# Edge sums of a relational network: from one stream on 125 weight columns to two streams on blocks of 64 and 61

## The reference

```
def _mgcn_conv(x, edge_index, edge_type, rel, W_in, W_out, W_loop, b, n):
    src, dst = (edge_index[0], edge_index[1])
    e = edge_index.shape[1]; half = e // 2
    m = x[src] * rel[edge_type]
    m = jnp.concatenate([m[:half] @ W_in, m[half:] @ W_out], 0)
    deg = jax.ops.segment_sum(jnp.ones((e,), x.dtype), dst, num_segments=n)
    norm = 1.0 / jnp.maximum(deg, 1.0)
    agg = jax.ops.segment_sum(m * norm[dst][:, None], dst, num_segments=n)
    return jnp.tanh(agg + x @ W_loop + b)
h = emb + res * _mgcn_conv(emb, ..., rel1, W_in1, W_out1, W_loop1, b1, n)
h = h + res * _mgcn_conv(h, ..., rel2, W_in2, W_out2, W_loop2, b2, n)
gnn = h @ mu_w + mu_b
...
xn = _layernorm(x)
x = x + gnn(xn, src, dst, edge_type) + mix(xn)   # mix: 4 layers of linear attention and a 256-1024-256 FFN
x = x + ffn(_layernorm(x))                       # shared MLP plus 4 experts, the best 2 weighted
```

## Time and profile before

| | |
|---|---|
| median of three runs | 1943.48 us |
| span of the profiled execution | 1937.8 us |
| TensorE busy | 1821.0 us (94%) |
| GpSimd busy | 1322.3 us (68%) |
| VectorE busy | 1248.8 us (64%) |
| ScalarE busy | 632.8 us (33%) |

### The profile page before, as it was taken

How to read it: one execution, slowest core, us unless ns; L and a number is a source line. 1 busy time by engine, 2 the same in 40 slices (tenths; PEclk the granted TensorE clock), 3 DMA queues, 4 the chain that set the end, 5 groups by cost and what they waited for, 6 DMA issues and landing times.

```text
span 1937.8 us, 28847 instructions
## 1 busy us (share of the span) xinstructions
PE 1821.0 (94%) x9176; PEld 1505.8 (78%) x9176; DVE 1248.8 (64%) x3345; ACT 632.8 (33%) x1552; POOL 1322.3 (68%) x1301
## 2 busy tenths in 40 slices
PE   2899899999899999999999789998899999999999
PEld 1567787887588888768888667876788888888998
DVE  6786465674855576486466645868765666654766
ACT  4452233343323333332333222332121211223443
POOL 6777777777777777777777757777777777770000
PEclk9999999999999999999999989999999999999999
DMA  9568666667776666687677856667766766661000
GB/s 274 177 198 258 203 191 206 186 202 222 243 209 199 204 194 198 208 249 214 193 218 220 274 190 229 190 200 224 229 182 215 209 199 200 190 181 17 15 28 28
DMA packets 194575, 371.44 MB, mean 192 GB/s; under 512 B 37993, under 2 KB 126095, under 8 KB 194430
## 3 DMA queue, kind: packets, MB, share of 16 engines
q0 software_dynamic: 77632, 223.91, 40.6%
q1 hardware_dynamic: 92228, 126.68, 19.9%
q10 hardware_dynamic: 24570, 19.04, 3.4%
HBM read 305.39 MB, written 64.95 MB: 191 GB/s over the span
## 4 chain that ended last, share of the span: by engine, by line
PE 80%; DVE 8%; issue 3%; DMA 3%; POOL 2%; SPq 2%; ACT 2%; DVEq 0%; ACTq 0%
PE ps_down L2765 16%; PE ps_hid L2753 16%; PE ps_seg L2629 15%; PE ps_kv L2662 5%; PE ps_x L2717 4%; PE ps_x L546 3%; PE ps_hid L3229 2%; PE ps_kv L3082 2%; POOL xg L959 2%; PE ps_hid L2682 1%; DVE xg L1055 1%; PE ps_kv L2795 1%; PE ps_down L2795 1%; DMA h_rows<-qT_all 1%; PE ps_hid L3220 1%
## 5 line engine op out<-in xcount | busy, mean ns | idle before, releaser
L959 POOL DMA_INDIRECT xg<-h_rows,idx_tab x416 | 437.2, 1051 | 143.3 <-issue 114.0
L906 POOL DMA_INDIRECT rg<-relation_rows,idx_tab x416 | 426.7, 1026 | 133.5 <-issue 126.1
L959 POOL DMA_INDIRECT xg<-xn_rows,idx_tab x416 | 423.4, 1018 | 131.9 <-issue 120.3
L2629 PE MATMUL ps_seg<-xg,hot 128*125 128x257 f32 x1664 | 414.8, 382 | 19.7 <-DVE xg L1055 19.5
L2753 PE MATMUL ps_hid<-hT,wff 128*128 128x250 f32 (+1 forms) x1920 | 368.3, 341 | 1.0 <-issue 0.8
L2629 PEld LDWEIGHTS ps_seg<-xg,hot 128*125 128x125 f32 x1664 | 305.3, 188 | 75.0 <-DVE xg L1055 19.2
L2765 PE MATMUL ps_down<-wff,gT 128*125 128x256 f32 x1600 | 363.6, 381 | 0.0
L2753 PEld LDWEIGHTS ps_hid<-hT,wff 128*128 128x128 f32 x1920 | 312.8, 189 | 37.9 <-issue 7.9
L1055 DVE TENSOR_TENSOR xg<-xg,rg 128x512 f32<-128x512 f32 x416 | 285.8, 687 | 70.8 <-DMA rg<-relation_rows,idx_tab 52.0
L2765 PEld LDWEIGHTS ps_down<-wff,gT 128*125 128x125 f32 x1600 | 295.2, 188 | 41.3
L2204 ACT ACTIVATE gT<-ps_hid,b1p 128x250 f32<-128x250 f32 (+1 forms) x480 | 177.8, 433 | 291.6 <-PE ps_hid L2753 291.5
(11 more groups left out here) (378 smaller groups left out, 2385.5 us busy)
## 6 DMA issues: line engine op xcount, KB each, us to landing
second_relation_rows<-rg SPq DMA_DIRECT2D x104, 512.0 KB, 4.1
rg<-second_relation_rows SPq DMA_DIRECT2D x104, 512.0 KB, 4.1
wff<-L_mix_W ACTq DMA_DIRECT2D x8, 1024.0 KB
rg<-relation_rows,idx_tab POOLq DMA_INDIRECT x416, 3.5
xg<-xn_rows,idx_tab POOLq DMA_INDIRECT x416, 3.2
xg<-h_rows,idx_tab POOLq DMA_INDIRECT x416, 3.6
h_rows<-qT_all SPq DMA_DIRECT2D x25, 112.0 KB
qrow<-h_rows ACTq DMA_DIRECT2D x25, 112.0 KB
```

The costliest lines, as they stand in the source:

```text
L906: pool.indirect_dma_start(rg[:, k, :], None, rel_d, bass.IndirectOffsetOnAxis(ap=idx_tab[:, step, 1:2], axis=0))\
L959: pool.indirect_dma_start(xg[:, k, 0:D], None, rows, bass.IndirectOffsetOnAxis(ap=idx_tab[:, step, 0:1], axis=0))\
L2629: ins = pe.matmul(ps_seg[u // UW % 2][0:T, 0:AW], hot[:, s % HOTS, :], xg[:, s % RING, :], start=s % WIN == 0, stop=s % WIN == WIN - 1)
```

## The change

The edges are cut into two streams, the first and the second half of the list (208 steps each). The nodes are cut the same way: tile t now holds 64 nodes of a first strip (nodes 64t on) and 61 of a second (1600 + 61t on), so that stream one fills partitions 0 to 63 of a tile and stream two partitions 64 to 124. A unit is four steps, two of each stream, and each step's one-hot is 64 columns wide. TensorE sums a pair of steps by two matmuls one behind the other, one with 64 weight columns to the lower partitions, one with 61 to the upper ones (L2735). For the nodes in which the streams overlap, 12 steps of a layer get one more matmul (L2740).

With it change: windows of 6 pairs and 97 masked adds a layer in place of 104, plus one plain one, at row numbers known when the program is built (no loads of row numbers); one-hots and products of four steps in one VectorE instruction each (208 and 208 where there were 416 and 416); a slot of the ring is released after four steps, not two; the relations are reloaded 4 blocks ahead, not 8; the tile products become two loop matmuls over the full width and four over the strips (L3190, L3193); rows move in three DMAs, not two; x comes back by a load and a VectorE add, so no `add_x` is left on GpSimd.

The order changes too: the passage stands behind (2,3), one group later, with 6 units (24 steps) among its tiles, behind every third; the second network layer starts with (2,4), and its last 104 steps are doled out over the experts' slots 1 to 12; 18 of the product slots move behind layer 3 as well, to the experts' slots 1 to 16.

```
-UNIT = 2
-WIN = 8
+UNIT = 4
+HOT_UNITS = 2
+WIN = 6
+STRIPS = ((0, 64), (64, T))
...
-STEPS_JOINT = (14, 14, 14, 36)
-STEPS_GROUP = ((20, 26, 24, 24, 24), (20, 24, 24, 24, 22), (18, 24, 68, 48, 54), (58, 58, 58, 56, 48))
-AMONG, AMONG_AT = 20, 2
-DENSE_LAYER, DENSE_GROUP = 2, 3
+STEPS_JOINT = (16, 16, 16, 32)
+STEPS_GROUP = ((16, 24, 24, 24, 24), (16, 24, 24, 24, 24), (16, 24, 24, 48, 48), (24, 52, 52, 52, 52))
+STEPS_LAST = 104
+AMONG, AMONG_AT, AMONG_EVERY = 6, 3, 3
+DENSE_LAYER, DENSE_GROUP = 2, 4
+LAG = 18
...
# TensorE, one unit
-                    for s in range(u * UNIT, (u + 1) * UNIT):
-                        ins = pe.matmul(ps_seg[u // UW % 2][0:T, 0:AW], hot[:, s % HOTS, :], xg[:, s % RING, :],
-                                        start=s % WIN == 0, stop=s % WIN == WIN - 1)
+                    for i in range(PER):
+                        now = u * PER + i
+                        for j, (a, z) in enumerate(STRIPS):
+                            part = j * PER + i
+                            ins = pe.matmul(ps_seg[bank_of(w)][a:z, 0:AW], hot[:, u % HOT_UNITS * UNIT + part, 0:z - a],
+                                            xg[:, u % RU * UNIT + part, :], start=now == r, stop=now == end - 1)
...
# TensorE, one tile's product
-                for k in range(n):
-                    ins = pe.matmul(out_rows, sums(k), weights[k // KC](k % KC), start=k == 0, stop=k == n - 1)
+                for c in range(KC):
+                    pe.matmul(bank_rows(0, T), sums(KC + c), wg[g][2][:, c, :], start=c == 0, stop=False)
+                for c in range(KC):
+                    for j, (a, z) in enumerate(STRIPS):
+                        ins = pe.matmul(bank_rows(a, z), sums(c)[:, a:z], wg[g][j][:, c, :], start=False, stop=c == KC - 1)
...
# the experts' slots on TensorE
+                for slot in slots[:len(slots) // 2]:
+                    dense_beside(slot)
...
+                upto(last_units(s, 0))
                 if s < NT:
                     experts_1(s)
...
+                upto(last_units(s, 1))
+                for slot in slots[len(slots) // 2:]:
+                    dense_beside(slot)
```

827 lines of the change are left out of this document (466 added, 361 removed).

## The result

The changed kernel takes 1985.66 us (median of four runs, 1978.38 to 1990.71) against 1942.67 for the kernel before: ratio 1.0233, 95% interval 1.0202 to 1.0265 (the quotient of the two medians is 1.0221). It is slower; 1859 was forecast, in a range from 1832 to 1925. The profiled execution is the slowest of the four, with a span of 1988.9 us.

What follows compares the result with a forecast made beforehand. TensorE was taken as the bound, with GpSimd equally pacing the first layer. Passage ends 1168, layer 3 starts 1286, experts 1609, slot 12 ends 1754, then 99: span 1853, plus 5.7 gives 1859 us; range 1832 to 1925.

Steps and rivals of the forecast that it cites:

- A step on TensorE: Edge matmuls on two column blocks: overlap makes a four-step unit take 1.08 us, 0.27 a step, where it was 0.435.
- First-layer gathers end at 1133: First network layer: GpSimd issues the same 832 gathers, so the last one ends at 1133 us as before.
- What costs nothing: List of edits taken as free, among them four-step one-hots and products on VectorE, saving time that nobody waits for.
- TensorE reaches the passage at 1078: Passage behind (2,3): TensorE gets there at about 1078 us, when GpSimd, at 1069, has 24 first-layer steps left.
- (2,4) 107: Group (2,4) with the joint: 85.5 us without edges plus 80 steps at 0.27 makes 107 us.
- layer 3 323: Mix layer 3, from 1286 to 1609 us: five groups sum to 315 us, with 8 added for waits.
- slots 1 to 12 145: Experts' slots 1 to 12: 130 us of TensorE work plus 15 us of waits, slot 12 ending at 1754.
- GpSimd is ahead by less than its ring: Start of the experts: TensorE arrives at 1609 us, and GpSimd has step 312 there at 1599.
- x's way back and the third DMA: x's DMAs leave GpSimd's queue, about 2 us each; each row move's third DMA, on SyncE's queue, is covered by the passage.
- No overlap: Rival: blocks do not overlap, a unit costs 1.74 us as before, extra matmuls add 53 us: 1997 us; chance 0.13.
- the first rival: Partial overlap, 0.35 us a step, or 0.217 us pauses between blocks and full width: 1905 us; chance 0.17.
- VectorE's edge work in the experts: Rival: VectorE and the experts' banks set slots 1 to 12, uncovered products and one-hots cost 43 us: 1902; chance 0.11.

Runs made afterwards that it cites:

- e6: Changed kernel with VectorE's product of a unit in two instructions of two steps instead of one of four: 1954.69 us, ratio 1.0091 to the kernel before.
- e8: Changed kernel with no edge steps beside the experts; layer 3's groups carry 64 and four times 68 steps: 2055.22 us, ratio 1.0603 to the kernel before.
- e13: e6 with second-layer gathers fetching 64 rows in place of 128: 1956.70 us, ratio 1.0111 to the kernel before.
- e4: Kernel before the change with units of four steps in place of two, no column blocks: 2042.79 us, ratio 1.0574 to the kernel before.
- e3: Changed kernel with units of two steps in place of four, and with them the product in two: 1991.26 us, ratio 1.0293 to the kernel before.
- e14: e3 with 56 steps beside the experts in place of 104, the others moved to layer 3: 1971.02 us, ratio 1.0163 to the kernel before.
- e17: Changed kernel; at layer 3's start ScalarE loads x and one h tile first, other tiles behind its first gelus: 1979.99 us, ratio 1.0198 to the kernel before.
- e18: Changed kernel with the edits of e6 and e17, layer 3's steps at even places and three units of one-hots: 1939.94 us, ratio 0.9998 to the kernel before.
- e1: Changed kernel with loops over steps and blocks exchanged in unit and tile product, same block's matmuls in succession: 1977.53 us, ratio 1.0218 to the kernel before.
- e5: Changed kernel with every edge and strip matmul over the full width, no blocks, same number of matmuls: 2052.64 us, ratio 1.0595 to the kernel before.
- e10: e6 with rows moved in two DMAs of 64 and 61 rows in place of three: 2189.34 us, ratio 1.1311 to the kernel before.

## Why the prediction was wrong

- **A step on TensorE: the size right, the mechanism not.** 1.02 to 1.11 us for the forecast 1.08. The forecast was five lengths of 0.216, with one block's first pass beside the other's second; the records show four, with both blocks' passes side by side, and some 0.09 us at each change of width, 0.18 a unit, which the sum put at nothing. That the two errors cancel is luck. The reading of the earlier trace rows went wrong because a modelled end behind the next start says nothing of a pause: the unit at 343.65 has such an end too (344.74, the next start 344.67), and the pause is there. The Trainium skill (TensorEngine Tiling (Array Packing), Key Properties) has a drain at each change of tiling mode, and this trace agrees that a change costs something, with 0.31 where 0.216 is usual.
- **First-layer gathers end at 1133: wrong, 1155.9.** The step that failed stands under "What costs nothing": the four-step product "saves VectorE time that nobody waits for". Nobody waits for it, but its length holds GpSimd's gathers up (e6), and GpSimd set the first layer's pace: the earlier trace rows had told that. 17 of the 23 us are longer gathers (437.7 and 429.5 us busy for 423.4 and 426.7). I costed the edit by its engine, not by what else its instruction touches.
- **TensorE reaches the passage at 1078, 8 us behind GpSimd: wrong, 1120** (1097 in e6). 21 to 23 us are the gathers. The rest is lag: TensorE starts its first group at 183.3 in place of 168.3, and at 63.06 busy of 64.60 us a group, with GpSimd at 24 x 2.69 = 64.6 (1.052 and 1.033 and two issues of 0.30 a step), it can't catch up. The passage itself took 83 us, 90 forecast; it ended at 1203, not near 1168, which was one of the signs named for being wrong. The first gather behind it came after 6.4 us, not 4.
- **(2,4) 107, layer 3 323, slots 1 to 12 145, the end 99 us: measured 127, 377, 156 and 113** (to the end of the span). PE busy is 109, 333, 140 and 98. In (2,4) the 107 held 9 us of idle time of the kernel before, and left out the 12 extra matmuls of a layer (L2740), which stand there: 24 instructions, some 5 us. In layer 3 the work was put at 315; a good part of the difference is the clock of 0.95, at which the FFN's 880 matmul instructions of this layer take 195.1 us (before, at 1.00, 185.2). The rest is idle time. What failed is the step "GpSimd is ahead by less than its ring", by which TensorE would hardly wait. By my own numbers 52 steps are 71 us on GpSimd, and TensorE needed 70.2: two engines with equal work, coupled by a ring of four units and by VectorE's order. GpSimd waited 84 us for slots, VectorE 58 for second-layer gathers (of the 129 us ahead of L1143), TensorE 44 in layer 3, some 24 of them behind a late gather. I added 8. That the equal pace makes them wait is argued from these rows and from e8; no run changed GpSimd's pace in the second layer (e13 hardly did). "Up to two steps longer" for the coarser release was the wrong measure too, if e4's 110 us, part of them by the long product, are a guide; in the changed kernel e3 and e14 don't show such a cost.
- **x's way back and the third DMA: mis-costed.** I looked at GpSimd's queue and SyncE's; eight of the 18 issues that stand ahead of the gelu are new ones on ScalarE's (x15 was x10, and x3 is new), and x is now waited for on VectorE. e17 and e18 put the place at 0.0035, 7 us.
- **The clock: not in the sum.** After 9 us of idle time TensorE came back at about half its clock, 0.54, as the rows of the changed kernel under e17 show; the FFN's matmuls of the whole kernel, whose number is the same, take 744 us in the changed kernel and 732 before.
- **The rivals.** No overlap is excluded (e1, e5). A pause at each change of width is real, but 0.09 us where the first rival took 0.217, and paid for by the fuller overlap. VectorE's edge work in the experts is real with units of two (e3, e14). With units of four the 15 us of waits added to slots 1 to 12 were about right (16.4 idle), though 9.6 of them are for the norm and only 5.1 for edge products; the 11 us beyond the forecast are busy time, at a clock of 0.93. What came true was not among the rivals: none asked what the change does to GpSimd's pace and to its coupling with TensorE, and "slower" had 0.13, all of it for no overlap.

A small slip in the prediction: GpSimd's waits for TensorE in the second layer are 41, not 35, so 12.7 us lie beyond the usual 0.30; the 1.37 a step stays.

In sum: start of the second layer 36 us late, (2,4) 20, layer 3 54, slots 1 to 12 11, the end 14, together 135 of the 136 us by which the span missed. e18 takes 50 of them back (46 by the medians) by removing the long product, the bunches and the issues; 86 stay, 21 as the late start (1200 for 1179) and 65 as idle time and clock behind it. Of these, 16.6 are waits for the norm and 10.7 the one for `kmax`. That the rest would go with a deeper ring, or with VectorE's products placed behind what TensorE needs first, was not tried and stays open.

## What to carry to other kernels

When TensorE's work is cut, take the next engine's pace for the same stretch and compare: here the two were within 2% of each other and shared a ring of four units, and more than half of the matmul time saved came back as waits on both sides. Merging instructions on an idle engine is not free: look for what runs slower while the long one executes. And issues of DMAs count on the queue of the engine that issues them, ahead of everything behind them.

## What the runs showed of the hardware that was not expected

- GpSimd's indirect gather of 128 rows, 0.95 us, took up to 2.1 us beside a 128x1024 product of VectorE (1.22 us); with two products of 0.687 the mean was back at 1.005 to 1.024. One long instruction is not the only thing that does it: the longest gather of the kernel before took 3.35 us (at 1239.11), beside a row of one-hots of 0.41 and products of 0.69 us without a pause.
- A gather of 64 rows takes 0.987 us on average, one of 128 rows 1.024 (e13): hardly anything of the price hangs on the number of rows.
- Matmuls on different column blocks start together even when the program puts two of the same block first (e1).
- With 61 rows in one DMA in place of 48 and 13 in two, the kernel was 235 us slower (e10 against e6).
